# A mixture-of-experts stage on one core: expert rows added to the output by indirect DMA instead of by scatter products, and the turns of the next group moved between experts

## The reference

```python
gates = softmax(xn @ Wg.T)                    # (B, 256, 8)
val, idx = top_k(gates over the 256 tokens)   # per batch and expert: 64 tokens
rows = xn[b, idx[b, e]]                       # (B, 8, 64, 128)
h = gelu(rows @ W1[e] + b1[e])                # 512 wide
y = (h @ W2[e] + b2[e]) * val[b, e]
out[b] = x[b];  out[b, idx[b, e]] += y        # for all e: a token can be chosen by several experts
```

## Time and profile before

| | us |
|---|---|
| median of 3 executions | 2515.89 |
| the profiled execution's own time | 2518.26 |
| its span in the trace | 2516.5 |
| TensorE busy (products) | 1978.0 (79%) |
| VectorE busy | 1928.1 (77%) |
| POOL busy | 1360.5 (54%) |
| ScalarE busy | 1262.5 (50%) |

### The profile page before, as it was taken

One profiled execution on the slowest core, in us unless ns is written; L12 is line 12 of the kernel. 1 busy time (PEld: TensorE's weight loads), 2 busy tenths in 40 slices (PEclk: granted clock), 3 DMA queues, 4 the chain that ended last, 5 costly groups with the idle time before them and its releaser, 6 DMA issues. The chain is left out here.

```text
span 2516.5 us, 43496 instructions
## 1 busy us (share of the span) xinstructions
PE 1978.0 (79%) x14556; PEld 1538.8 (61%) x14556; DVE 1928.1 (77%) x3471; ACT 1262.5 (50%) x2982; POOL 1360.5 (54%) x1106
## 2 busy tenths in 40 slices
PE   1478888888888888888888888888888836758699
PEld 0466666666666666666666666666666624647477
DVE  8989899999988999989989888999998511512223
ACT  2256555555555555655655556666655413303132
POOL 5656666666666666666666666666663253142200
PEclk9889889999989999989998899999898857879799
DMA  3000000000000000000000000000000011020110
GB/s 93 5 5 10 9 8 8 8 8 8 10 8 10 8 10 8 10 8 8 8 8 8 8 8 8 8 8 8 8 6 7 5 38 36 11 67 14 54 34 26
DMA packets 64577, 39.56 MB, mean 16 GB/s; under 512 B 9350, under 2 KB 60431, under 8 KB 64528
## 3 DMA queue, kind: packets, MB, share of 16 engines
q1 hardware_dynamic: 60386, 30.51, 4.3%
q0 software_dynamic: 4096, 8.40, 1.2%
q10 hardware_dynamic: 46, 0.00, 0.0%
HBM read 26.31 MB, written 12.58 MB: 15 GB/s over the span
## 5 line engine op out<-in xcount | busy, mean ns | idle before, releaser
L774 PE MATMUL pa<-ident,arena 128*128 128x128 f32 x4096 | 530.7, 286 | 56.8 <-DVE arena L652 52.5
L774 PEld LDWEIGHTS pa<-ident,arena 128*128 128x128 f32 x4096 | 503.0, 201 | 74.0 <-DVE arena L652 35.3
L1059 PE MATMUL pb<-ident,arena 128*128 128x128 f32 x1536 | 290.6, 302 | 157.0 <-ACT arena L954 142.0
L1059 PEld LDWEIGHTS pb<-ident,arena 128*128 128x128 f32 x1536 | 187.6, 153 | 275.4 <-issue 187.6
L954 ACT ACTIVATE arena<-pb 128x384 f32<-128x384 f32 x512 | 252.5, 493 | 188.2 <-PE pb L1059 152.1
L680 POOL TENSOR_TENSOR arena<-state,c_cross 128x448 f32<-128x448 f32 x128 | 203.3, 1608 | 206.1 <-DVE state L541 201.3
L672 POOL TENSOR_TENSOR arena<-arena,neg_half 128x32 f32<-128x32 f32 x64 | 264.9, 4158 | 83.7 <-DVE arena L518 83.7
L652 POOL TENSOR_TENSOR arena<-arena 128x1024 f32<-128x1024 f32 x64 | 150.3, 2348 | 195.2 <-PE pa L774 195.2
L947 ACT ACTIVATE arena<-pd,arena 128x256 f32<-128x256 f32 x512 | 245.1, 479 | 0.0
L652 DVE TENSOR_TENSOR arena<-arena 128x1024 f32<-128x1024 f32 x192 | 235.9, 1254 | 2.6 <-PE pa L774 2.2
L946 ACT ACTIVATE arena<-pd,arena 128x128 f32<-128x128 f32 x512 | 188.8, 369 | 67.1 <-DVE arena L834 65.0
(11 more groups left out here) (250 smaller groups left out, 4403.0 us busy)
## 6 DMA issues: line engine op xcount, KB each, us to landing
x_land<-in_L_attn_query SPq DMA_DIRECT2D x32, 128.0 KB, 2.1
arena<-in_L_attn_query SPq DMA_DIRECT2D x32, 128.0 KB, 2.1
x_scratch<-x SPq DMA_DIRECT2D x32, 128.0 KB, 1.8
xn_scratch<-xn_d SPq DMA_DIRECT2D x32, 128.0 KB, 1.8
arena<-x_scratch SPq DMA_DIRECT2D x16, 256.0 KB
out_x<-arena SPq DMA_DIRECT2D x16, 256.0 KB
w<-in_L_ffn_W SPq DMA_DIRECT2D x1, 2048.0 KB
arena<-xn_scratch,arena POOLq DMA_INDIRECT x128
```

The costliest lines, as they stand in the source:

```text
L774: mm = pe.matmul(pa[:, t, c * P:c * P + P], wprod[:, k % NWP, j * 128:j * 128 + 128], ident[:, :], start=(j == 0), stop=(j == NH - 1))
L1059: mm = pe.transpose(pb[:, j * P:j * P + P], p_raw[:, s % 3, j * P:j * P + P], ident[:, :])
```

## The change

- `out` takes the place of `x3_d`: `sync_d` stores the residual to the output, and the loads of `x3`, the final additions and the final stores of the expert stage are gone, with `spread`, `token_ids`, `spread_at` and `vector_spread`.
- After each expert, `gpsimd_add` issues one indirect DMA for each of the four pairs, which adds 128 rows of `y_exp` to their rows in `out`. It waits for VectorE's result and, pair by pair, until the add of the expert before has landed (`c_put_m`), for two experts may add to one row.
- VectorE adds the bias in one instruction and then multiplies by the gate, in place. `y_exp` has four slots (`KEPT`) in turn; a slot is written again when its four adds have landed.
- `gpsimd_experts` puts the gathers of the next group's pair `e` ahead of the adds of expert `e`, for `e` of 0 to 3. `x_sel` has two copies, and the turn of pair `m` of the next group stands on TensorE between `up(4 + m)` and `down(3 + m)`; ScalarE's copies stand after the gelus of expert `4 + m`.
- `tensor_lists` and `vector_lists` of the second half move from the end of group 0 to the start of group 1. `vector_lists` makes 8 small copies instead of 12.

```diff
         def sync_d(sp, b):
-            sp.dma_start(tiles(x3_d[b]), x3[:, :, :]).then_inc(S("x3_gone"), 16)
+            sp.dma_start(tiles(out[b]), x3[:, :, :]).then_inc(S("x3_gone"), 16)
...
+        def gpsimd_add(gp, g, e):
+            gp.wait_ge(S("c_yexp"), NX * g + e + 1)
+            for m in range(NM):
+                if g or e:
+                    gp.wait_ge(S(f"c_put_{m}"), 16 * (NX * g + e))
+                c = (g * NM + m) * NX + e
+                gp.indirect_dma_start(out.rearrange("b n e -> (b n) e"), bass.IndirectOffsetOnAxis(ap=chosen_row[:, c:c + 1], axis=0),
+                                      y_exp[:, e % KEPT, m, :], None, compute_op=ALU.add).then_inc(S(f"c_put_{m}"), 16)
+
+        def gpsimd_experts(gp, g):
+            for e in range(NX):
+                if e < NM and g < NG - 1:
+                    gpsimd_gather(gp, (g + 1) * NM + e)
+                if g == 0 and e == 0:
+                    gp.wait_ge(S("x3_gone"), 16 * B + 1)
+                gpsimd_add(gp, g, e)
...
         def vector_experts(v, g):
...
-                if e < NM:
-                    vector_spread(v, g, e)
...
-                for side in range(2):
-                    y = v.tensor_tensor(y_exp[HALF[side], r, :, side ^ q, :], ...
-                y.then_inc(S("c_yexp"), 1)
+                if n >= KEPT:
+                    for m in range(NM):
+                        v.wait_ge(S(f"c_put_{m}"), 16 * (n - KEPT + 1))
+                y = y_exp[:, e % KEPT, :, :]
+                v.wait_ge(S("c_y"), n + 1)
+                v.tensor_tensor(y, pa[:, e % 2, :].rearrange("p (m n) -> p m n", m=NM),
+                                b2_all[:, e, :].unsqueeze(1).broadcast_to([P, NM, E]), ALU.add).then_inc(S("c_plus"), 1)
+                v.wait_ge(S("c_plus"), n + 1)
+                v.tensor_tensor(y, y, gates_of[:, :, e].unsqueeze(2).broadcast_to([P, NM, E]), ALU.mult).then_inc(S("c_yexp"), 1)
-            for m in range(NM):
-                v.wait_ge(S(f"c_x3_in_{m % 2}"), ...)
-                v.wait_ge(S("c_scattered"), NM * g + m + 1)
-                (two additions of x3 and the scatter's bank)
...
         def tensor_experts(pe, g):
             pe.wait_ge(S("c_xsel"), GRP * g + GRP)
-            pe.wait_ge(S("c_added"), NM * g + 2)
+            if g == 1:
+                tensor_lists(pe, 1)
...
                 if e < NX:
                     up(e)
...
+                if NX - NM <= e < NX and g < NG - 1:
+                    tensor_turn(pe, g + 1, e - (NX - NM))
                 if e:
                     down(e - 1)
-            (the turns of the next group, and for each pair the scatter products, L1393)
```

More of the change, by code:

```diff
@@ L229, in build @@
         gate_p_all = sb("gate_p_all", [P, T, B * NX])
+        KEPT = 4
+        NM = GRP // 2
         x_rows = [third(f"x_rows_{i}", [P, NX, E]) for i in range(4)]
-        x_sel = third("x_sel", [P, NX, GRP, CAP])
+        x_sel = [third("x_sel_0", [P, NX, GRP, CAP])]
         g_rows = third("g_rows", [P, HALVES, 256])
@@ L238, in build @@
         b2_all = third("b2_all", [P, NX, E])
-        token_ids = third("token_ids", [P, T * P])
         row_of_batch = third("row_of_batch", [P, B // 2, NX // 2, 2])
         chosen_row = third("chosen_row", [P, B // 2 * NX], U32)
-        spread_at = third("spread_at", [P, B // 2 * NX])
-        spread_gate = third("spread_gate", [P, B // 2 * NX])
+        chosen_gate = third("chosen_gate", [P, B // 2 * NX])
         h_act = third("h_act", [P, 2, NF, GRP * CAP])
[L245 to L248, removed]
+        x_sel.append(third("x_sel_1", [P, NX, GRP, CAP]))
+        y_exp = third("y_exp", [P, KEPT, NM, E])
         raw = start("raw", [P, 384])
@@ L1146, in half_lists @@
         def half_lists(h, kind):
-            bank = pa[:, 0, :] if h == 0 else pd[:, 0, :]
+            bank = pa[:, 0, :] if h == 0 else pc[:, :]
             return bank[:, kind * R:kind * R + R]
@@ L1197, in vector_half @@
             yield
-        CHOSEN = 12
+        CHOSEN = 8
         PAIRS = B // 2 // HALVES
-        NUMBERS = 1 + 2 * HALVES
+        NUMBERS = 2 * HALVES
         def vector_lists(v, h):
@@ L1261, in scalar_turn @@
                 act.wait_ge(S("c_turned"), GRP * g + 2 * m + i + 1)
[L1262 to L1280, removed]
-            for m in range(NM):
[L1282 to L1295, removed]
+                act.activation(x_sel[g % 2][:, 4 * i:4 * i + 4, 2 * m:2 * m + 2, :].rearrange("p e b s -> p e (b s)"),
+                               row_bank(g, i).rearrange("p (e n) -> p e n", e=4), ACT.Copy).then_inc(S("c_xsel"), 1)
         def vector_experts(v, g):
@@ L1314, in vector_experts @@
-            assert next(half, None) is None
[L1315 to L1318, removed]
-                v.wait_ge(S("c_scattered"), NM * g + m + 1)
[L1321 to L1325, removed]
@@ L1338, in scalar_experts @@
                     act.activation(h_act[:, e % 2, f, :], pd[:, f, :], ACT.Gelu_apprx_tanh, bias=b1[:, e, f:f + 1])\
                         .then_inc(S("c_gelu"), 1)
-            if g < NG - 1:
-                for m in range(NM):
-                    scalar_turn(act, g + 1, m)
+                if e >= NX - NM and g < NG - 1:
+                    scalar_turn(act, g + 1, e - (NX - NM))
         def tensor_experts(pe, g):
             pe.wait_ge(S("c_xsel"), GRP * g + GRP)
-            pe.wait_ge(S("c_added"), NM * g + 2)
+            if g == 1:
+                tensor_lists(pe, 1)
@@ L1480, in _ @@
             sp.wait_ge(S("xn4_gone"), 16 * B + 1)
-            sp.wait_ge(S("b_gate"), B)
-            for g in range(NG):
-                sync_experts(sp, g)
-            for i in range(2):
-                sp.wait_ge(S(f"out_gone_{i}"), 16 * (NM // 2) * NG + 1)
+            for m in range(NM):
+                sp.wait_ge(S(f"c_put_{m}"), 16 * NX * NG)
         @block.gpsimd
@@ L1497, in _ @@
             together(g, stages, LAST, POOL_ORDER)
-            for k in range(NM, NG * NM):
-                gpsimd_gather(g, k)
+            for k in range(NG):
+                gpsimd_experts(g, k)
         @block.scalar
@@ L1529, in _ @@
                 v.sem_inc(S(name), 1)
-            for name, count in PAIRS_FREE.items():
-                v.sem_inc(S(name), count)
             v.wait_ge(S("pool_setup"), POOL_SETUP)
```

72 lines of the change are left out of this document (28 added, 44 removed).

## The result

In the runs of the forecast the changed kernel takes 2482.8 us (median of 4, 2476.6 to 2487.8) against 2516.0 us for the kernel before (median of 4, 2507.0 to 2522.4): a ratio of 0.9876, interval 0.9845 to 0.9907. The profiled execution took 2484.73 us with a span of 2482.9, 33.6 less than before. The forecast was 2480.

The account below looks back on a forecast made before the run. Holds beside POOL's 32-gather bursts bound the kernel (102.0 us). Walk: group 3 starts at 2408, experts end 2464, landing 2474, longer adds 2482; -34.5 against the span 2516.5, so 2515.9 - 34.5, rounded to 2480; range 2412 to 2600.

Parts of the forecast that it names:

- 102.0 us of holds: Expert stage, kernel before: excess of three long stretches beside POOL's 32-gather bursts, 29.5 + 36.2 + 36.3 us.
- all but untouched: Layers before 2110.8 us: the change hardly affects them, so the case is decided in the last 405.7 us.
- I take 1.4, near the gather: POOL's slot per indirect add: 1.4 us, between 1.25 (a gather's slot) and 2.2 us.
- the 0.15 us put down for the two waits: POOL, each add: 0.15 us, an estimate, for its two waits, on top of the gather's 1.25 us slot.
- The walk's holds: Expert groups: TensorE stands 18 and 13 us in group 0; groups 1 and 2 take 102 us each.
- A pause of POOL starts the count anew: POOL's bursts: any pause restarts the burst's time count; chosen, since no row shows a short pause.
- the rule: Beside POOL's bursts: signals older than 10 us into one are held until 5 us after it; TensorE stands after 17 us.
- rival (1): Expert stage: short bursts hold nothing, POOL's own queue binds; -97 us, 2418 us; chance 0.14.
- rival (2): Expert stage: POOL never pauses long enough to release TensorE; slower, 2536, 2568 or 2618 us, 2568 taken; chance 0.38.
- The 102 of the middle groups: Expert groups 1 and 2: 102 us each, with results held during POOL's adds and gathers.
- The last pair's gathers are out 15 us before its turn: Moved turns, experts 4 to 7: gathered rows come in time, so they cost nothing beside the turns.
- Landing: End of the kernel: the last adds land 2.5 to 3 us after issue; chain on a pair binds above about 7.

Follow-up runs that it names:

- chip A: Chip, not on record, of the forecast's runs and profile; results held; changed kernel 2482.8 us against 2516.0 us for the kernel before.
- E: Chip of the last session, both kernels unaltered; results held; changed kernel 2483.2 us, kernel before 2513.5 us in 8 runs, ratio 0.987.
- chip C: Chip where nothing is held; changed kernel unaltered 2456.3 us against 2388.9 us for the kernel before, ratio 1.027.
- B: Chip where nothing is held; kernel before unaltered 2387.6 us; changed kernel with plain writes in place of additions 2392.2 us.
- the half-and-half kernel: Changed kernel with pairs 0 and 1 scattered by TensorE's products, pairs 2 and 3 by DMA adds: 2364.5 us against 2381.0 us for the kernel before.

## Why the forecast's number was right and its walk was not

The forecast was 2480 and the result 2482.8, but that they lie so close is luck: one term was too small, another should not have been there, and the two nearly cancel.

**The bound of the kernel before: right for its chip.** The 102.0 us of holds were there and were sized within 3 us. Read wrongly was their reach: the first group's run of 32 gathers had also stopped TensorE for 23.68 us inside layer 1, which I left out as "all but untouched" since the change keeps that burst.

**"I take 1.4, near the gather": the step that failed.** The slot is 1.86 us, 128 x 0.46 = 59 us more of POOL's time. The upper end of the bounds, the gather's slot and its busy part once more, was 2.2. Its form, a price of the addition on top of the gather's slot, is what was measured, at two thirds of the size: a plain write costs the gather's 0.97 us and the addition 0.60 more. That this is a second read, from which the prediction had its upper end, is not shown; what the runs show is 1.58 against 0.97 us of issue and 144 against 32 packets. Nor does a run show the 0.15 us put down for the two waits: POOL idles 0.30 us before an add with "issue" as before a gather (37.5 us over 123 adds, 38.6 over 127 gathers).

**The walk's holds: wrong.** It had TensorE stand 18 and 13 us in group 0 and results held in groups 1 and 2. No stand of a product with "issue" occurred in the stage on chip A or E, and results came late only once on A, by 5.7 us of VectorE's idle time, and twice on E, by 5.9 us and, for ScalarE, 1.7. "A pause of POOL starts the count anew" can't save the rule: POOL did not pause at all for 353 us, and by the rule everything should have been held. What the runs show is narrower: on a holding chip 32 gathers in a row hold, and runs of at most eight gathers between adds, back to back, hold one or two results, for 5.9 us at most. Whether it is the run of gathers or something that adds let drain is open.

**What bound instead: rival (1)'s mechanism at rival (2)'s slot.** The sum of rival (1) with the measured slot, 2127 + 88 x 1.25 + 128 x 1.86 + 3 = 2478, is the span within 5 us, and with the measured first add and end, 2124 + 110 + 238 + 6 = 2478, the rest being adds and gathers that take a little more, 1.88 and 1.27 us in the mean. So POOL's own queue is the time, at 32 x (1.25 + 1.86) = 99.5 us a group.

**Two errors cancelled.** Starts of groups lie 81.6, 99.7 and 101.9 us apart; forecast 94, 102 and 102, and 2.4 more each for adds of 1.4 us. So the last group starts 283 us into the stage and not 305 (298 + 7.2), without the holds. It then takes 91.3 us and not 67, since the span goes on for 35 us after the last product, with POOL's 16 late adds, where "some 10 us after the last product" was forecast. -22 and +25. The 102 of the middle groups was right for the wrong reason: 80 us of POOL and three pauses of 7 for held results, against 99.5 us of POOL and no hold.

**"The last pair's gathers are out 15 us before its turn": wrong.** With 7.5 us of adds in each expert's 7 the gathers are late and TensorE waits 76.5 us in ten stands, all named as gathered rows. It costs nothing of its own, since POOL is the bound either way (the moved turns undone: no change).

**Landing.** 2.5 to 3 us after the last issue was forecast, 6.0 measured to the end of the span; what fills them isn't shown. On chip C, where the trace has landings, an add lands 3.3 us (median) after its issue and a gather 2.5. The chain of adds on one pair did not bind at these landings, with 0.9 us of POOL's idle time on chip A put down to it in all; that it would above about 7 us was an estimate, and no run came to it.

**Still open: what makes a chip hold.** The five sessions fall in two classes with nothing between, 2505 to 2523 and 2379 to 2396 us for the kernel before, and each stays in its class through all of its runs (31 on B, 17 on E). B to E were used in one session each, and A's chip isn't on record, so chip and session can't be told apart. Beside a burst of 32 gathers ScalarE waits 3.96 us at most on chip C and stops for 34.66 us on A and 34.64 on E; no run shows where it is held. Runs of 1, 8 and 16 gathers in the kernel before, the changed kernel with 32 gathers ahead, and the half-and-half kernel met only chips without the hold; what they would do on the others wasn't tried.

## What to carry to other kernels

Where a wide part of the gain is the end of a stall that no semaphore explains, time the kernel before on a second chip before trusting it: here the stall was worth some 128 us in two sessions and was absent in three, and with it the sign of the change turned. An addition by indirect DMA is not free because it takes no product and no vector instruction: 128 rows of 512 bytes take a queue slot of 1.86 us on POOL, and with the gathers of 1.25 us that is a bound of its own, to be summed before the rest is walked. When two engines can do the same job, give each the share it has time for: half of the scatter on each was faster than all of it on either, by 0.8% and 3.7%, on the one chip where it ran.

## What was not expected of the hardware

- An indirect DMA costs POOL nearly the same to gather and to write (0.96 and 0.975 us for 128 rows of 512 bytes, and 0.30 between two of them), and 1.58 with an addition, with single ones up to 2.06 us on chip A. In packets a write is 32 and an addition 144.
- POOL issued indirect DMAs without a pause for 353 us beside TensorE's products, gathers and adds in turn, and this held one result on A and two on E, for 5.9 us at most. On the same two, beside 32 gathers in a row, ScalarE stops for 34.6 us, and on A TensorE takes 85.6 us for the experts beside them, where a quiet group takes 56.1.
- The same program, with the same data, has two times 5% apart that go with the chip or the session and not with the execution: none of the executions in any of the five sessions left its class.
